# Causal masks by VectorE in place of TensorE, and ones-products beside the value products, in a fused attention and expert layer

## The reference

```
scores = jnp.einsum('bhqd,bhkd->bhqk', q, k) / jnp.sqrt(jnp.float32(DH))
causal = jnp.tril(jnp.ones((s, s), dtype=bool))
scores = jnp.where(causal[None, None], scores, -jnp.inf)
attn = jax.nn.softmax(scores, axis=-1)
out = jnp.einsum('bhqk,bhkd->bhqd', attn, v)
```

## Time and profile before

| | |
|---|---|
| median of 3 runs | 2754.18 us |
| the profiled execution's own time | 2747.54 us |
| its span | 2745.9 us |
| mean granted clock of TensorE | 0.942 |
| PE busy | 2458.5 us (90%) |
| PEld busy | 1537.2 us (56%) |
| DVE busy | 1493.4 us (54%) |
| ACT busy | 1001.6 us (36%) |
| POOL busy | 1001.1 us (36%) |

### The profile page before, as it was taken

One profiled execution on the slowest core, in us unless ns is written; L12 is line 12 of the kernel. 1 busy time (PEld: TensorE's weight loads), 2 busy tenths in 40 slices (PEclk: granted clock), 3 DMA queues, 4 the chain that ended last, 5 costly groups with the idle time before them and its releaser, 6 DMA issues. The chain is left out here.

```text
span 2745.9 us, 35084 instructions
## 1 busy us (share of the span) xinstructions
PE 2458.5 (90%) x13112; PEld 1537.2 (56%) x13112; DVE 1493.4 (54%) x2366; ACT 1001.6 (36%) x1288; POOL 1001.1 (36%) x592
## 2 busy tenths in 40 slices
PE   5996799999999999999999869999479999999950
PEld 5774444444444444444444357777367777777740
DVE  3665575565566655556666064444635555555535
ACT  2332144444445444454444522122023333333310
POOL 0000056465556646464565733221121111111026
PEclk8998599999999999999999989999669999999975
DMA  3776301313131221413120134432235445454449
GB/s 115 256 269 214 86 22 47 78 32 78 32 78 32 62 63 47 118 42 78 28 76 9 26 96 138 138 107 92 81 96 169 155 155 170 146 180 136 128 146 374
DMA packets 178737, 301.76 MB, mean 110 GB/s; under 512 B 23616, under 2 KB 65728, under 8 KB 178624
## 3 DMA queue, kind: packets, MB, share of 16 engines
q1 hardware_dynamic: 159360, 242.54, 29.0%
q0 software_dynamic: 14656, 49.29, 5.7%
q10 hardware_dynamic: 4608, 8.39, 0.8%
HBM read 199.65 MB, written 100.27 MB: 109 GB/s over the span
## 5 line engine op out<-in xcount | busy, mean ns | idle before, releaser
L756 DVE TENSOR_REDUCE b_mpart<-b_mx 128x1 f32<-128x512 f32 (+3 forms) x1280 | 745.8, 608 | 490.9 <-PE b_mx L848 318.5
L790 ACT ACTIVATE b_pt<-b_st 128x1024 f32<-128x1024 f32 (+3 forms) x640 | 565.2, 896 | 611.3 <-PE b_st L872 351.7
L637 POOL TENSOR_TENSOR b_acc<-b_acc,b_pt 128x1024 f32<-128x1024 f32 (+1 forms) x256 | 593.6, 2341 | 148.4 <-ACT b_pt L790 148.3
L848 PE MATMUL b_mx<-b_k,b_q 96*128 96x512 f32 (+2 forms) x1280 | 559.3, 445 | 51.7 <-DVE b_mt L764 25.9
L872 PE MATMUL b_st<-b_q,b_k 97*128 97x512 f32 (+2 forms) x1280 | 515.7, 418 | 22.7 <-ACT b_pt L790 11.8
L848 PEld LDWEIGHTS b_mx<-b_k,b_q 96*128 96x128 f32 x1280 | 250.5, 196 | 347.1 <-DVE b_mpart L756 282.6
L872 PEld LDWEIGHTS b_st<-b_q,b_k 97*128 97x128 f32 x1280 | 245.2, 194 | 173.5 <-issue 101.9
L890 PE MATMUL b_ob<-b_pt,b_v 128*32 128x512 f32 (+3 forms) x2560 | 302.5, 545 | 0.5 <-ACT b_pt L790 0.5
L637 POOL TENSOR_TENSOR b_acc<-b_pt 128x1024 f32<-128x1024 f32 x48 | 113.2, 2377 | 459.8 <-ACT b_pt L790 459.8
L61 PE MATMUL e_fb<-e_xh,e_w_guh 128*128 128x512 f32 (+1 forms) x552 | 220.8, 400 | 1.5 <-DVE e_xl L1698 1.5
L63 PE MATMUL e_fb<-e_xl,e_w_guh 128*128 128x512 f32 (+1 forms) x552 | 218.5, 396 | 0.0
(11 more groups left out here) (224 smaller groups left out, 3535.7 us busy)
## 6 DMA issues: line engine op xcount, KB each, us to landing
scr_y<-e_y SPq DMA_DIRECT2D x23, 1024.0 KB, 5.0
b_q<-scr_qh SPq DMA_DIRECT2D x64, 256.0 KB, 4.3
b_k<-scr_kh SPq DMA_DIRECT2D x64, 256.0 KB, 4.0
e_gu<-in_L_ffn_w_gate_dram SPq DMA_DIRECT2D x23, 704.0 KB, 6.2
e_gu<-in_L_ffn_w_up_dram SPq DMA_DIRECT2D x23, 704.0 KB, 7.5
e_d<-in_L_ffn_w_down_dram SPq DMA_DIRECT2D x23, 512.0 KB, 7.6
a_xin<-in_L_attn_x_dram POOLq DMA_DIRECT2D x8, 1024.0 KB, 6.0
scr_qh<-a_qh SPq DMA_DIRECT2D x8, 1024.0 KB, 4.5
```

Source lines behind the costliest of these rows:

```text
L637: g.tensor_tensor(out[:, :, lo:], so_far[:, :, lo:], pt[n % NPB][:, :, lo:], ALU.add).then_inc(s_add, 1)
L756: v.tensor_reduce(mpart[u % 2][:, t, h, c:c + 1], mxb[i % NMX][:, 0:w], AX.X, ALU.max).then_inc(s_red, 1)
L790: act.activation(pt[n % NPB][:, :, lo:], stb[n % NST][:].rearrange("k (h q) -> k h q", h=2)[:, :, lo:], ACT.Exp, scale=SCALE).then_inc(s_e ...
L848: ins = pe.matmul(bank[:, 0:max(w, 2 * P)], qb[0:KR, h, q * CH + t * P:q * CH + (t + 1) * P], kb[0:KR, h, at:at + max(w, 2 * P)], start=Tr ...
```

## The change

Three edits go together. The mask matmuls are gone from TensorE. For the scores VectorE adds a triangle `sooner` (128 x 128, f32) to both heads' blocks in the score banks, and ScalarE's exp of a diagonal step waits for that. For the maxima the reduction of a chunk on the diagonal becomes a `tensor_tensor_reduce` that adds `later` and takes the maximum, and writes the sum, which nobody reads, to `unread`. And the ones-products of a pair m are issued in step 2m + 3, right behind its value products; `room` counts them there.

```diff
@@ attention_plan
         if p:
-            work += 4 * width
-        elif kt not in POOL_TILES[q]:
-            work += 4 * width
+            work += 4 * width * (1 + (kt not in POOL_TILES[q]))
@@ phase_attention
+    def masked(n):
+        u, q, kt, p = steps[n]
+        return TPC * PAIRS * u + PAIRS * (kt - TPC * q) + p
+
+    def item_shares(n):
+        here, there = upto[n - 1] if n else start, upto[n]
+        return [here + (there - here) * k // 3 for k in range(4)]
...
-        causal = al.sb("b_causal", [P, P], mybir.dt.bfloat16)
-        identb = al.sb("b_identb", [P, P], mybir.dt.bfloat16)
+        sooner = al.sb("b_sooner", [P, P])
+        later = al.sb("b_later", [P, CH])
+        unread = [al.sb(f"b_unread{n}", [P, CH], mybir.dt.bfloat16) for n in range(2)]
...
@@ VectorE
-                    v.tensor_reduce(mpart[u % 2][:, t, h, c:c + 1], mxb[i % NMX][:, 0:w], AX.X, ALU.max).then_inc(s_red, 1)
+                    part = mpart[u % 2][:, t, h, c:c + 1]
+                    if c == q:
+                        v.tensor_tensor_reduce(unread[i % 2][:, 0:w], mxb[i % NMX][:, 0:w], later[:, CH - w:], 1.0, -3e38,
+                                               ALU.add, ALU.max, part).then_inc(s_red, 1)
+                    else:
+                        v.tensor_reduce(part, mxb[i % NMX][:, 0:w], AX.X, ALU.max).then_inc(s_red, 1)
...
+                def mask(n):
+                    u, q, kt, p = steps[n]
+                    d = kt - TPC * q
+                    block = stb[n % NST][:].rearrange("k (h q) -> k h q", h=2)[:, :, d * P:(d + 1) * P]
+                    v.wait_ge(s_st, n + 1)
+                    v.tensor_tensor(block, block, sooner[:].unsqueeze(1).to_broadcast([P, 2, P]), ALU.add).then_inc(s_msk, 1)
+
                 for n in range(NS):
-                    for i in range(upto[n - 1] if n else start, upto[n]):
+                    here, _, some, there = item_shares(n)
+                    for i in range(here, some):
+                        if stream[i][0] == "max":
+                            partial_max(i)
+                    if steps[n][2] >= TPC * steps[n][1]:
+                        mask(n)
+                    for i in range(some, there):
                         if stream[i][0] == "max":
                             partial_max(i)
@@ ScalarE
-                    act.wait_ge(s_st, n + 1)
+                    if kt >= TPC * q:
+                        act.wait_ge(s_msk, masked(n) + 1)
+                    else:
+                        act.wait_ge(s_st, n + 1)
@@ TensorE
-                                        kb[0:KR, h, at:at + max(w, 2 * P)], start=True, stop=(c < q))
-                        if c == q:
-                            ins = pe.matmul(bank[:, w - P:w], identb[:], causal[:], start=False, stop=True)
+                                        kb[0:KR, h, at:at + max(w, 2 * P)], start=True, stop=True)
...
-                                    qb[:, h, q * CH + lo:(q + 1) * CH], start=True, stop=d < 0)
-                    if d >= 0:
-                        ins = pe.matmul(stb[n % NST][:, j * CH + d * P:j * CH + (d + 1) * P], causal[:], identb[:],
-                                        start=False, stop=True)
+                                    qb[:, h, q * CH + lo:(q + 1) * CH], start=True, stop=True)
...
-                    if n % 2 == 0 and n >= 4:
-                        count_ones((n - 4) // 2)
                     if n % 2 and n >= 3:
                         values((n - 3) // 2)
+                        count_ones((n - 3) // 2)
```

More of the change, by code:

```diff
@@ L594, in phase_attention @@
         s_st = al.sem("b_scores_made")
+        s_msk = al.sem("b_scores_masked")
         s_exp = al.sem("b_exp_made")
@@ L611, in _ @@
                 make_identity(g, ident, s_cst, 0)
-                g.memset(causal[:], 0.0).then_inc(s_cst, 1)
+                g.memset(sooner[:], 0.0).then_inc(s_cst, 1)
                 g.wait_ge(s_cst, 3)
-                g.affine_select(out=causal[:], in_=causal[:], compare_op=ALU.is_ge, fill=-1e30, base=0,
-                                pattern=[[-1, P]], channel_multiplier=1).then_inc(s_cst, 1)
[L616 to L620, removed]
+                g.affine_select(out=sooner[:], in_=sooner[:], compare_op=ALU.is_ge, fill=-1e30, base=0,
+                                pattern=[[1, P]], channel_multiplier=-1).then_inc(s_cst, 1)
+                g.memset(ones[:], 1.0).then_inc(s_cst, 1)
+                g.memset(later[:], 0.0).then_inc(s_cst, 1)
+                g.wait_ge(s_cst, 6)
+                g.affine_select(out=later[:, CH - P:], in_=later[:, CH - P:], compare_op=ALU.is_ge, fill=-1e30, base=0,
+                                pattern=[[-1, P]], channel_multiplier=1).then_inc(s_cst, 1)
                 for i, n in enumerate(pool_ops):
@@ L765, in _ @@
                 v.wait_ge(s_set, NSET)
+                v.wait_ge(s_cst, NCST)
                 for i in range(start):
@@ L921, in _ @@
                 for n in range(NS):
-                    here, there = upto[n - 1] if n else start, upto[n]
-                    some = [here + (there - here) * k // 3 for k in range(1, 4)]
+                    here, *some = item_shares(n)
                     score(n, 0)
@@ L933, in _ @@
                     score(n, 1)
-                    for i in range(some[1], there):
+                    for i in range(some[1], some[2]):
                         item(i)
@@ L939, in _ @@
                 values(NS // 2 - 1)
-                count_ones(NS // 2 - 2)
                 count_ones(NS // 2 - 1)
```

## The result

The changed kernel takes 2768.65 us (median of 8 runs, 2762.75 to 2771.14) against 2752.69 for the kernel before (8 runs). The ratio is 1.0057, 95% interval 1.0042 to 1.0071: 16 us slower. The forecast was +53 and a range from 2720 to 2862. The sign was right, the size three times too large, and the experiments show that two of its terms had the wrong sign: that the sum still had the right one was partly luck.

The account below looks back on a forecast made before the run. It took TensorE (PE) to bound the kernel, busy 90% of the span. Terms 38 + 24 - 9 = +53 us put the profiled execution at about 2800 and the median at 2807; range 2720 to 2862, for 8 in 10.

Parts of the forecast that it names:

- What bounds it: Whole kernel: PE busy 90% of the span, DVE 54%; PE 98% busy in the middle head groups.
- the link that I read as tight: Key tile 13, query chunk 3: next odd score starts 0.07 us after exp's end; later exp costs +0.8 us.
- What TensorE gets back: Removing 1024 mask matmuls, mean 0.07 us each, returns between 0 and 72 us.
- What VectorE gets: 256 additions at 0.425 us, 109 us, plus accumulator work; DVE in attention goes from 744 to about 904 us.
- The accumulator term: Second DVE row behind each of 512 adds with maximum, 0.1 us each: 51 us, between 0 and 76.
- Where the additions stand: Diagonal steps: additions between score and exp delay exps; net +1.2 us a unit, 32 units: +38 us.
- tile 15's link: Last diagonal odd step of the unit: shortest exp and larger slack, so no delay: 0.
- What the moved ones-products cost: Even steps off the diagonals lose their ones-products and turn short: 80 at 0.3 us, +24 us.
- The rest: 248 item masks outside diagonal steps return 9 us; Pool's new constants ahead of the phase count inside 0.
- A: Rival, chance 0.20: VectorE absorbs the additions in idle time, exps have slack; 48 us faster, 2706.

Follow-up runs that it names:

- e4: Kernel before with only the masks of the maxima moved to VectorE; score masks stay on TensorE: 2719.89 us, 0.9893.
- e2: Kernel before with both kinds of masks on VectorE, ones-products and their count in `room` as before: 2721.04 us, 0.9903.
- e7: The early kernel: changed kernel with the score's second half, and VectorE's addition, issued ahead of value and ones-products: 2712.74 us, 0.9871.
- e13: Changed kernel without score masks; VectorE does 256 one-input reductions of 0.42 us instead, which the exp does not await: 2710.07 us, 0.9857.
- e14: Changed kernel with an unused VectorE reduction of 0.42 us ahead of each of the 256 additions: 2849.89 us, 1.0369.
- e15: Early kernel (e7) with an unused VectorE reduction of 0.42 us ahead of each of the 256 additions: 2740.30 us, 0.9961.
- e1: Kernel before with only the ones edit: ones-products right behind the value products and `room` counting them there; masks on TensorE: 2738.72 us, 0.9963.
- e16: Kernel before with ones-products placed beside the value products, but `room` and so the plan of items as before; masks on TensorE: 2735.43 us, 0.9949.
- e5: Changed kernel with `room`, and so the plan of items, as before; ones-products stay beside the value products: 2750.31 us, 1.0000.
- e10: Kernel before with only the new `room`, and so the new plan of items; ones-products stay in the even step: 2763.31 us, 1.0041.
- e9: Changed kernel without score masks; VectorE does its 256 additions on an SBUF buffer of its own, which the exp does not await: 2787.05 us, 1.0124.

## Why the forecast was wrong

- **What bounds it**: right, TensorE in attention (in the changed kernel still busy 1160.9 of its 1298 us). But the link that I read as tight was not typical: of the 96 odd diagonal steps of the six middle groups 7 were tight, 4 of them that of key tile 13 in units of q = 3. In units of q = 0 the slack was 1.17 to 1.80 us in the median.
- **"What TensorE gets back"**: the mean of 0.07 us a mask as an upper end held up for the maxima (e4: 30 us / 512 = 0.06, net of VectorE's part). But I then credited 248 masks with 9 us and those ahead of the odd scores with 0.8 us a unit. That was too little: the mask edits alone are worth 29 us (e2), with the additions already paid. What I read behind a mask stands in the loads of the kernel before: the next product's weight load starts 0.08 us after the product of 512 columns that it follows (1109.55 and 1109.47), with no mask ahead of that product 0.01 (1072.57 and 1072.56). The pace of the weight load behind 256 columns was my estimate; it came near: with no mask the next product of 512 columns starts 0.22 us after the one of 256 (changed kernel), with a mask 0.27, so the 0.04 return. But the product of 512 behind it gives back 0.08 as well (0.32 to 0.24; medians, six middle groups), which I had counted only behind 512 columns.
- **"What VectorE gets"**: each price right (0.425, 0.686). The accumulator term of 51 us was wrong: the read is 83 ns and ends with its main instruction. The total was 820 us and not 904; the rest of the difference goes with queued DVE instructions that overlap (an addition recorded as 0.42 is followed 0.33 later, 1126.54 to 1126.87). In the trace of the changed kernel 512 rows of 83 ns stand behind the 512 adds with maximum, at next to no cost.
- **"Where the additions stand" (+38)**: the first step that failed. The mechanism is shown (timeline above, e7, e13, e14 against e15). But as the price of the mask edits alone it has the wrong sign: without the ones edit the diagonal steps of the six middle groups became 2.5 us a group shorter (e2, 57.0 in place of 59.5, from the starts of their scores). I took the sum of one unit of q = 3, +1.2 us, for all 32, and the others had more slack. With the ones edit the link term does show: these steps became 3.1 us longer a group, 25 over eight groups in place of 38, and tile 15's link, which I had set at 0, was tight in 22 of 24 cases. That the ones-products had covered the exp I had priced for tile 14 alone.
- **"What the moved ones-products cost" (+24)**: the second step that failed. "The move takes no work away, so it has no gain to set against this" is wrong: side by side the two cost 0.14 us less, and alone the edit is 11 us faster (e1), its place 15 (e16). Short even steps do cost, as I said: off the diagonals 84 of 144 links are tight in e1 and 54 before. But the saving outweighs them. In the changed kernel, masks and all, these steps became 2.2 us shorter a group in place of 1.9 longer (24 / 8 less 9 / 8).
- **The rest**: the start, "inside 0", and the first group at a lower clock were 11 of the 23 us. The first group's part comes with the plan (202.7 us, and 196.9 in e5 with the old plan), which I had given no price. Of the start's 5.2 us Pool's constants may be little: e10 and e16, which have the old ones, begin their scores at 300.0 and 300.3.
- Of the rivals, A's condition (additions within 0.1 us of the score's end in most odd steps) was not met: it holds for 25 of 128 odd diagonal steps, and for 49 in e2. Still its result, additions hidden and a gain, is what e2 shows with the ones-products left where they were, for there the exps had slack to give. I had not asked what one edit does to the slack of the other.

So +53 was made of +29 for the masks and +24 for the ones-products, where each alone measured -29 and -11. Neither price was right; the loss of 16 us is those two gains and an interaction of 56 us, most of which the forecast did not have.

## What to carry to other kernels

When two edits touch the same link, price each with and without the other: work that is moved away from behind a producer is slack taken from it. Before giving an engine work on such a link, look for an order that issues the producer (here the second half of a score) ahead of long independent work; that made the same instructions 2% faster. An order of work that fills a wait can be worth more than the work that another order saves: the ones-products beside the values save 20 us, and moving them back made the changed kernel 39 us faster. And before the price of one link is taken for all, count how many are like it.

## What the runs showed of the hardware

- An accumulator read behind an add with maximum: recorded 83 ns, no added time (changed kernel: 0.56 us for both over 384 columns; a plain reduce before, 0.554).
- A DVE addition with both inputs in SBUF took 1.35 us in the mean and up to 2.58 where an instruction of GpSimd overlapped it, 0.42 where none did (e9). With its first input in PSUM none of 256 took over 0.433, and 99 of them ran beside GpSimd (changed kernel).
- Value products and ones-products of the same pair of steps (four heads, 512 columns) hold PE for 1.86 us back to back (e1), and 1.00 each apart (before).
- The granted clock of the six middle groups was 0.95 with a reduction of 0.42 us added in each diagonal step (e14), where the changed kernel had 1.00; in the early kernel the same reductions left it at 0.99 (e15).
- With the plan alone changed, the first group's granted clock was 0.85 in place of 0.91 (e10).
